# The expert stage of an attention-and-experts layer in blocks of 128 slots instead of groups of 256

## What is computed

```python
scores = xf @ router_w.T                      # 4096 x 8
top_v, top_i = jax.lax.top_k(scores, 2)
routing_w = jax.nn.softmax(top_v, axis=-1)
for e in range(8):
    w_e = jnp.sum(jnp.where(top_i == e, routing_w, 0.0), axis=-1)
    h = jax.nn.gelu(xf @ expert_w1[e].T, approximate=False)   # 256 -> 1024
    out = out + h @ expert_w2[e].T * w_e[:, None]             # 1024 -> 256
```

## Time and profile before

| | |
|---|---|
| median of 3 runs | 933.75 us (933.5 to 934.82) |
| span of the profiled execution | 930.5 us |
| attention and routing, to the first matmul of an expert | 488.9 us |
| expert stage on PE, to the last result read | 918.1 us |
| scatters behind it, to the end | 930.5 us |
| PE busy over the span | 93% |

### The profile page before, as it was taken

The page is one execution under the profiler, slowest core; times in us unless marked ns, Lnnn a source line. Parts: engine busy times, 40 slices in busy tenths (PEclk is TensorE's granted clock), DMA queues, the critical chain, the costliest instruction groups (busy, mean ns, idle before and its releaser), DMA issues. The chain is left out here.

```text
span 930.5 us, 22118 instructions
## 1 busy us (share of the span) xinstructions
PE 869.7 (93%) x6720; PEld 715.7 (77%) x6721; DVE 515.2 (55%) x1523; ACT 419.4 (45%) x1135; POOL 404.6 (43%) x408
## 2 busy tenths in 40 slices
PE   3899999999999999998559999999999999999993
PEld 1677777777777777776448989999989989999983
DVE  5766787667776677667963333334433333444331
ACT  3544454444545455443445444444444444444440
POOL 3444344433444344432452444454444444444532
PEclk9877777777777777777789999999999999999998
DMA  5212222222212222110001233223223322232222
GB/s 162 82 58 86 91 90 61 75 90 90 78 63 85 90 90 77 60 58 23 6 23 30 46 51 53 49 45 50 46 45 46 54 52 45 45 51 45 45 40 23
DMA packets 39834, 55.79 MB, mean 60 GB/s; under 512 B 5440, under 2 KB 33216, under 8 KB 39808
## 3 DMA queue, kind: packets, MB, share of 16 engines
q0 software_dynamic: 14976, 20.46, 13.4%
q1 hardware_dynamic: 24832, 35.02, 12.0%
HBM read 36.58 MB, written 18.87 MB: 60 GB/s over the span
## 5 line engine op out<-in xcount | busy, mean ns | idle before, releaser
L364 PE MATMUL bank<-stage,w1h 128*128 128x256 f16 x1248 | 208.3, 274 | 1.5 <-DVE stage L1170 1.5
L1106 PE MATMUL bank<-w2h,pt 128*128 x624 | 170.1, 273 | 1.6 <-DVE spare L1177 1.6
L364 PE MATMUL bank<-stage,w1l 128*128 128x256 f16 x624 | 171.0, 274 | 0.0
L1106 PE MATMUL bank<-w2l,pt 128*128 x624 | 170.1, 273 | 0.0
L1106 PE MATMUL bank<-w2h,spare 128*128 x624 | 170.1, 273 | 0.0
L364 PEld LDWEIGHTS bank<-stage,w1h 128*128 x1248 | 122.7, 98 | 16.6 <-issue 1.9
L1143 ACT ACTIVATE pt<-ss 128x512 f16<-128x512 f32 x78 | 44.8, 621 | 175.8 <-PE bank L1106 175.8
L750 PEld LDWEIGHTS bank<-val,pt 128*128 128x128 f32 x512 | 86.5, 213 | 34.6 <-issue 9.0
L750 PE MATMUL bank<-val,pt 128*128 128x16 f32 x512 | 111.3, 296 | 0.2 <-DVE pt L954 0.2
L1048 POOL DMA_INDIRECT out<-res,rows_to x40 | 63.8, 1594 | 107.9 <-DVE rows_from L1163 45.0
L1048 POOL DMA_INDIRECT out<-attn,rows_to x38 | 60.7, 1597 | 98.5 <-DMA out<-attn,rows_to 57.6
(11 more groups left out here) (198 smaller groups left out, 1920.8 us busy)
## 6 DMA issues: line engine op xcount, KB each, us to landing
stage<-w1c SPq DMA_DIRECT2D x16, 512.0 KB, 3.9
stage<-w2c SPq DMA_DIRECT2D x16, 512.0 KB, 3.5
xin<-x SPq DMA_DIRECT2D x32, 128.0 KB, 2.1
xn_rows<-xn SPq DMA_DIRECT2D x32, 128.0 KB, 1.7
xb<-x SPq DMA_DIRECT2D x32, 128.0 KB, 2.1
out<-res SPq DMA_DIRECT2D x32, 128.0 KB, 1.8
xin<-xn_rows,rows_from POOLq DMA_INDIRECT x40, 2.8
out<-res,rows_to POOLq DMA_INDIRECT x40, 3.8
```

The costliest lines, as they stand in the source:

```text
L364: ins = pe.matmul(dst, lhs(a, k), rhs(c, k), start=(n == 0), stop=(n == len(terms) - 1))
L1106: ins = pe.matmul(bY[h][:, 0:D], (hh, hl)[a][:, f, h * P:(h + 1) * P], (w2h, w2l)[c][:, DS(which * (FC * D) + f * D, D)], start=(f == a == ...
```

## The change

G becomes 128, so a unit of work is a block of 128 slots of one expert: NG = (8192 + 8·127) // 128 = 71 blocks, all of them always run. NB, the number of columns of the tables, goes from 78 to 71. The routing shifts by 7 bits instead of 8 and is otherwise the same.

In the stage, one block has one gather, 2 transposes, 48 matmuls of the first layer with 128 moving columns, 24 of the second with 256, and one scatter. Psum banks 0 and 7 hold the transposed rows in turn, and the hidden layer has two pairs of banks. Hidden values and their halves have two homes each, and gathered rows, results and their row numbers four; semaphores count ahead by 4. Loops have four blocks in a body, four blocks ahead and three behind: 4 + 16·4 + 3 = 71. The order of steps on PE is unchanged: `first(k+1)`, `turn_rows(k+2)`, `second(k)`.

The diff, cut to its core (the classes of indices, the names of semaphores, and POOL's part are left out; POOL's waits are described above and are the same for one gather and one scatter in each block):

```diff
-G = 2 * P
+G = P
 NG = (TOK * TOPK + E * (G - 1)) // G
-NB = G // P * NG
+NB = NG
...
-            then(dve, dve.tensor_scalar(nbi, nbi, 8, None, ALU.arith_shift_right))
+            then(dve, dve.tensor_scalar(nbi, nbi, 7, None, ALU.arith_shift_right))
...
+        FH = FC // 2
+        bX, bH, bY = (bank[0], bank[7]), (bank[1:3], bank[3:5]), bank[5:7]
+        xg, yg = [xin[0], xin[1], xb[0], xb[1]], [res[0], res[1], attn[0], attn[1]]
...
+        hid = [[view(buf, q * FH * G, FH * G) for q in range(2)] for buf in (ss, small)]
+        hh = [view(pt, m * (FC * G // 2), FC, G, dt=F16) for m in range(2)]
+        hl = [view(spare[0], m * (FC * G // 2), FC, G, dt=F16) for m in range(2)]
...
             @block.tensor
...
+                def turn_rows(k, off):
...
+                    n, m = k.four(off), k.two(off)
+                    pe.wait_ge(gathered[n], k.dma_done(off))
+                    pe.wait_ge(e["xgl_in"], k.done(off - 2))
+                    for c in range(KC):
+                        c0 = c * P
+                        ins = pe.transpose(bX[m][:, c0:c0 + P], xg[n][:, c * P:(c + 1) * P], ident[:])
                     ins.then_inc(e["xgt"], 1)
...
+                def first(k, off):
...
+                    which = pe.value_load(expert_of[0:1, DS(k.at(off), 1)], min_val=0, max_val=E - 1)
+                    pe.wait_ge(e["xgl_in"], k.done(off))
+                    xt = (xh[m], xl[m])
                     for f in range(FC):
+                        q = f // FH
+                        if f % FH == 0:
+                            pe.wait_ge(e[f"hid{q}"], k.done(off - 2))
+                        ins = three(pe, bH[m][q][:, f % FH * G:(f % FH + 1) * G],
                                     lambda a, c: (w1h, w1l)[a][:, DS(which * (KC * F) + (c * F + f * P), P)],
                                     lambda a, c: xt[a][:, c, :], range(KC))
...
+                def second(k):
+                    m = k.two(0)
+                    which = pe.value_load(expert_of[0:1, DS(k.at(0), 1)], min_val=0, max_val=E - 1)
+                    pe.wait_ge(e["y_in"], k.done(-2))
+                    for f in range(FC):
+                        if f % FH == 0:
+                            pe.wait_ge(e[f"hl{f // FH}"], k.done(0))
+                        for a, c in ((0, 0), (0, 1), (1, 0)):
+                            ins = pe.matmul(bY[m][:, 0:D], (hh, hl)[a][m][:, f, :],
+                                            (w2h, w2l)[c][:, DS(which * (FC * D) + f * D, D)],
+                                            start=(f == a == c == 0), stop=(f == FC - 1 and a == 1))
+                    ins.then_inc(e["y_ps"], 1)
+
+                def step(k):
+                    first(k, 1)
+                    turn_rows(k, 2)
+                    second(k)
...
             @block.scalar
...
+                    m = k.two(off)
+                    for q in range(2):
+                        act.wait_ge(e[f"h{q}"], k.done(off))
+                        act.wait_ge(e[f"hl{q}"], k.done(off - 2))
+                        act.activation(hid[m][q], bH[m][q][:], ACT.Gelu, scale=UN_XW).then_inc(e[f"hid{q}"], 1)
+
+                def step(k):
+                    m = k.two(0)
+                    act.wait_ge(e["y_ps"], k.done(-2))
+                    for q in range(2):
+                        act.wait_ge(e[f"hid{q}"], k.done(0))
+                        act.activation(half(hh[m], q), hid[m][q], ACT.Copy, scale=HS).then_inc(e[f"hh{q}"], 1)
+                    gelu(k, 1)
+                    rows_hi(k, 2)
...
             @block.vector
...
+                def step(k):
+                    m, n = k.two(0), k.four(0)
+                    for q in range(2):
+                        dve.wait_ge(e[f"hh{q}"], k.done(0))
+                        dve.scalar_tensor_tensor(out=half(hl[m], q), in0=hid[m][q], scalar=HS, in1=half(hh[m], q),
                                                  op0=ALU.mult, op1=ALU.subtract).then_inc(e[f"hl{q}"], 1)
+                    rows_of(k, 3)
+                    rows_lo(k, 2)
+                    if k.has(-4):
+                        wait_scattered[k.two(-4)](scattered[k.two(-4)])
+                    dve.tensor_copy(row_to[n], slot_row[:, DS(k.at(0), 1)]).then_inc(e["to_in"], 1)
+                    dve.wait_ge(e["y_ps"], k.done(0))
+                    dve.tensor_scalar(yg[n][:], bY[m][:, 0:D], slot_gate[:, DS(k.at(0), 1)], UN_HW,
+                                      ALU.mult, ALU.mult).then_inc(e["y_in"], 1)
```

More of the change, by code:

```diff
@@ L975, in _ @@
                 route_onehots(dve)
[L978 to L987, removed]
@@ L1021, in block_kernel, with blocks, half @@
+        def blocks(run, emit):
+            for j in range(4):
+                emit(Block(0, j))
+            with run.Fori(1, (NG - 3) // 4) as i:
+                for m in range(4):
+                    emit(Block(i, m))
+            for j in range((NG - 3) // 4 * 4, NG):
+                emit(Block(j // 4, j % 4))
+        def half(ap, q):
+            return ap[:, q * FH:(q + 1) * FH, :].rearrange("p f n -> p (f n)")
         with nc.Block() as block:
@@ L1023, in _, with gather @@
             def _(pool):
[L1024 to L1028, removed]
+                wait_rows, wait_y = stepper(pool, "rows_value", 1), stepper(pool, "y_value", LEAD + 1)
+                def gather(k, off):
+                    if not k.has(off):
                         return
-                    n, _k = slot(i, m, ahead)
-                    pool.wait_ge(e["from_in"], upto(i, m, ahead))
+                    n = k.four(off)
+                    pool.wait_ge(e["from_in"], k.done(off))
@@ L1032, in gather @@
                     wait_rows(e["xgt"])
[L1033 to L1050, removed]
+                    pool.indirect_dma_start(out=xg[n][:], out_offset=None, in_=xn_rows,
+                                            in_offset=bass.IndirectOffsetOnAxis(ap=row_from[n], axis=0))\
+                        .then_inc(gathered[n], 16)
@@ new lines, in step @@
+                def step(k):
+                    gather(k, 3)
+                    n = k.four(0)
+                    pool.wait_ge(e["to_in"], k.done(0))
+                    if k.has(-1):
+                        pool.wait_ge(scattered[k.two(-1)], k.dma_done_of_two(-1))
+                    wait_y(e["y_in"])
+                    pool.indirect_dma_start(out=out, in_=yg[n][:], in_offset=None, compute_op=ALU.add,
+                                            out_offset=bass.IndirectOffsetOnAxis(ap=row_to[n], axis=0))\
+                        .then_inc(scattered[k.two(0)], 16)
@@ L1052, in _ @@
                 for n in range(3):
[L1053 to L1056, removed]
+                    gather(Block(0, 0), n)
+                blocks(pool, step)
+                for n in range(2):
+                    pool.wait_ge(scattered[n], 16 * ((NG + 1 - n) // 2))
             @block.tensor
             def _(pe):
-                for n in ("xgt", "h0", "h1", "h2", "h3", "y_ps0", "y_ps1"):
-                    pe.sem_inc(e[n], 2)
@@ L1122, in rows_hi @@
+                def rows_hi(k, off):
+                    if not k.has(off):
                         return
[L1123 to L1126, removed]
+                    m = k.two(off)
+                    act.wait_ge(e["xgt"], k.done(off))
+                    act.wait_ge(e["h1"], k.done(off - 2))
+                    act.activation(xh[m].rearrange("p k n -> p (k n)"), bX[m][:, 0:D], ACT.Copy,
@@ L1139, in step @@
-                def step(i, m):
-                    act.wait_ge(e["y_ps1"], upto(i, m, -1))
-                    for q in range(4):
-                        act.wait_ge(e[f"hid{q}"], upto(i, m))
-                        act.activation(quarter(hh, q), hid[q], ACT.Copy, scale=HS).then_inc(e[f"hh{q}"], 1)
-                    gelu(i, m, 1)
-                    rows_hi(i, m, 2)
-                rows_hi(0, 0, 0)
-                gelu(0, 0, 0, between=lambda: rows_hi(0, 1, 0))
-                groups(act, step)
+                    m = k.two(off)
@@ L1165, in rows_lo, with rows_of @@
-                def rows_lo(i, m, ahead):
-                    if beyond(i, m, ahead):
+                for n in ("xgl_in", "hl0", "hl1", "y_in", "from_in", "to_in"):
+                    dve.sem_inc(e[n], LEAD)
+                wait_scattered = [stepper(dve, f"scattered{n}_value", 16, 16) for n in range(2)]
+                def rows_of(k, off):
+                    if not k.has(off):
+                        return
+                    n = k.four(off)
+                    dve.tensor_copy(row_from[n], slot_row[:, DS(k.at(off), 1)]).then_inc(e["from_in"], 1)
```

158 lines of the change are left out of this document (56 added, 102 removed).

## The result

The changed kernel takes **1061.7 us** (median of 4 runs, 1061.41 to 1062.12) against 933.62 us of the kernel before in the same runs: a ratio of 1.1365, 95% interval 1.1342 to 1.1388. It is 128 us slower. The forecast was 1083 us, range 1050 to 1120. The profiled execution took 1061.75 us, its span 1060.0.

What follows compares the result with a forecast made beforehand. TensorE's sequencer was taken to bound the changed kernel: 487.4 us to the first matmul plus 71 x 8.22 = 583.6, with small corrections 1072; 7.1 behind and 3.25 outside the span give 1082, stated 1083; range 1060 to 1110, 8 in 10 1050 to 1120.

Steps and rivals of the forecast that it cites:

- The reading: Expert stage: TensorE's sequencer, hidden behind the array's 10.91 us a group, needs 8.22 us a block against the array's 5.50.
- the rivals of the array, the stream and the waits: Array binds: 892 us, chance 0.07; short matmuls don't stream: about 982 us, 0.04; another wait or nothing changed: 0.01.
- The walk: TensorE's sequencer working through one block's addresses, value loads, waits and loop end: 8.22 us, 71 times, 583.6 us.
- the wait and the issue of four transposes, now two: 0.5: Term of the walk: from the first layer's end to the second load of the expert's number, 0.5 us a block.
- The array's 5.50 us: PE's array work a block: 2.66 first layer, 0.22 two transposes, 2.62 second layer; 390.5 us for 71 blocks.
- the rival's 892 us: Rival that the array binds at 5.50 us a block and the kernel is faster: 892 us, chance 0.07.
- Ahead and behind: Outside the blocks: first matmul moves from 488.9 to 487.4 us; 7.1 us follow the last matmul, no scatter queues.
- Outside the span: Difference between the profiled span 930.5 and the runs' median 933.75 us before, 3.25 us, added to the forecast.
- Loop bodies: Branch at a four-block body's end kept at 0.5 us; 1 us more for each of 16 bodies allowed in the range.
- the clock's rival: An array with gaps may be granted clock 0.50, 10.8 us a block: about 1130 us, chance 0.06.
- The signs: Expected in the changed profile: results 8.2 us apart, register pairs 0.24 to 0.25 apart, gaps before each `first` and `second`.

Runs made afterwards that it cites:

- The fixed addresses: Changed kernel with expert 0's weights at fixed addresses in both layers, output wrong: 895.9 us, ratio 0.9613 to the kernel before.
- the cut columns: Changed kernel with the first layer's moving columns cut from 128 to 64 or 96: 1068.4 us with 64, 1061.9 us with 96.
- the longer walk in the kernel before: Kernel before, groups of 256, with 32 more register operations and two more loads of the expert's number a group: 1024.6 us beside 934.52.
- the run with the second layer fixed: Changed kernel with fixed weight addresses (expert 0) in the second layer alone: 973.4 us, expected 925; ratio 1.0443 to the kernel before.
- the last experiment: Changed kernel with a branch every two blocks that uses one set of first-layer addresses for both when their expert is the same: 1016.2 us.

## Why the prediction was right, point by point

- *The reading.* That the sequencer's walk is hidden behind 10.9 us and comes out above 5.5 us was right. The fixed addresses (-166 us), the cut columns (no gain), and the longer walk in the kernel before (+90) each show it from another side; the rivals of the array, the stream and the waits are out.
- *The walk, 8.22 us forecast, 7.93 measured.* The terms that carry it held: 0.8 for load to first address (704.2 to 705.0), 3.9 for 16 pairs, 0.7 (forecast 0.85) for the second load (709.1 to 709.8), 1.95 for 8 pairs. The most mis-sized one is "the wait and the issue of four transposes, now two: 0.5": from the wait at 708.9 to the load at 709.1 it is 0.2 us in these rounded rows and 0.13 by the starts in the trace. This row was read where four transposes stood, and only about 0.1 was taken off for two. All terms together, 0.29 us over 71 blocks are 21 us, about the whole distance between forecast and result.
- *The array's 5.50 us* was 5.52 with fixed addresses, and the rival's 892 us was 896.
- *Ahead and behind.* The first matmul came at 486.1 us, forecast 487.4. The end was under-estimated: the last result is 1049.59, the span ends at 1060.0, 10.4 us and not 7.1. The last block has no `first` of a next one ahead of it, so its result follows the one before by 4.2 us and its scatter queues after all (POOL's timeline):

```profile
1046.78 1.76 POOL L1064 DMA_INDIRECT out<-res,rows_to  x1 [5.84 <-DVE res L1203]
1051.50 1.55 POOL L1064 DMA_INDIRECT out<-attn,rows_to  x1 [2.96 <-DMA out<-res,rows_to]
```

- *Outside the span* 1.7 us lie, not 3.25. The 3.25 set the span of one execution against the median of others; the profiled execution of the changed kernel has 1061.75 us and a span of 1060.0. Together: 1083 - 1.3 - 21 + 3.3 - 1.6 = 1062.
- *Loop bodies.* The end of a loop body costs about what was counted, 8.40 - 7.77 = 0.6 us once in four blocks against 0.5, and 17 pieces of program were loaded in the whole run. The 16 us allowed for it were not needed.
- *The clock* stayed at 1.00, as forecast; with half the columns it did not. The row that the clock's rival leans on was misread: from 206.2 to 212.9 us PE is busy for all of the 6.70 us, so it doesn't show that gaps bring 0.50, and it speaks against "without gaps it is granted 1.00". That the changed kernel kept its 1.00 followed from no row of the kernel before.
- *The signs.* Results 7.9 us apart, the even pace of the register operations, scatters that wait for results, and idle time put down to issue came as forecast. Matmuls of the first layer don't come in threes with a gap but as two and one, each behind its own register operation. And PE's idle time lies ahead of `second` (32.6 us from 520 to 1000 us); ahead of `first` it is 8.3 us, since there the array is still busy with the second layer before.
- *What the argument lacked.* It gave issue no price of its own. That does not matter for the change, where nearly every load and matmul rides behind a register operation, but it mis-sized the run with the second layer fixed by 48 us.

## What to carry to other kernels

Before making tiles of a loop smaller, add up the sequencer's own rows between two rounds (register operations, loads of run-time values, branches) as a second walk beside the array's; it is invisible as long as it is shorter, and it does not shrink with the tile when the number of addresses stays the same. Here it is 0.12 us for each distinct run-time address plus 0.7 to 0.8 us for each value loaded, and another 0.5 us a block for waits, semaphores and the loop. So the tile may shrink only until the array's work per round comes down to that sum. Where the gain is wanted all the same, take addresses out of the round; 896 us with fixed ones shows what they hold back.

## What the runs showed of the hardware that was not expected

- A register operation of TensorE's sequencer takes about 0.12 us from start to start, though its own length is 0.032 or 0.046, whether one load and one matmul go out behind it or two and two. What fills the rest, no row shows. The pace is the same with the array at either clock. The Trainium skill ("Advanced Engine Details and Errata", Clock Domains) has the sequencer of TensorE at 1.2 GHz beside an array at up to 2.4; that the rows don't change with the granted clock agrees with a clock of its own.
- Loads and matmuls at fixed addresses took some 0.015 us each to issue where 48 of them follow the wait, and 0.025 us each on average in the 96 of the last experiment; that a full queue is the reason is inferred from the counts above.
- At 896 us the array streams matmuls of 128 columns, each with its own load of 128 columns, at 0.056 us, 48 in a row in every block for 350 us, with POOL scattering and ACT and DVE reading banks beside it.
- The first jump over the second of two long bodies and the first jump into it held the sequencer for 3.9 and 4.1 us in the last experiment, later branches for 0.07 to 0.21. From 540 to 551 us, around the end of the 8.7 us in which PE stood idle, the granted clock was 0.53.
